# Forty-eight products of the identity at the head of TensorE's program for the experts

## The reference

```python
x = x + xattn(layernorm(x), ctx, Wq, Wk, Wv, Wo, bo)      # 16 heads of 64
x = x + causal_attention(layernorm(x), wq, wk, wv, wo)    # 16 heads of 64
y = layernorm(x)
probs = softmax(y @ router)                               # 8 experts
top, idx = top_k(probs, 2); gates = softmax(top)
for each token and each of its two experts e:
    h = silu(y @ gate[e]) * (y @ up[e])                   # 256 -> 512
    x += gates * (h @ down[e])                            # 512 -> 256
```

## Time and profile before

| | us |
|---|---|
| median of three runs | 2300.44 (2297.36 to 2302.71) |
| the profiled execution | 2298.02 |
| its span, first to last instruction | 2296.3 |
| TensorE busy in it | 2176.0 (95%) |
| VectorE, ScalarE, GpSimd busy | 1555.2, 1301.2, 914.2 |
| third stage, from 1925.92 | 370.4 |

### The profile page before, as it was taken

One profiled execution on the slowest core, in us unless ns is written; L12 is line 12 of the kernel. 1 busy time (PEld: TensorE's weight loads), 2 busy tenths in 40 slices (PEclk: granted clock), 3 DMA queues, 4 the chain that ended last, 5 costly groups with the idle time before them and its releaser, 6 DMA issues. The chain is left out here.

```text
span 2296.3 us, 56727 instructions
## 1 busy us (share of the span) xinstructions
PE 2176.0 (95%) x19008; PEld 1980.3 (86%) x19008; DVE 1555.2 (68%) x3525; ACT 1301.2 (57%) x3925; POOL 914.2 (40%) x1409
## 2 busy tenths in 40 slices
PE   6999999999999999999996999999999994999996
PEld 5899999999999999999995899999999983888885
DVE  6666676767676666667654888888888874444442
ACT  5555555555555555555553777777677762545442
POOL 3333333333333333333332225555555554444443
PEclk9999999999999999999997999999999996999998
DMA  4000000000000000000005200000000003444434
GB/s 120 22 20 28 9 27 18 27 11 25 27 18 27 9 27 18 27 9 27 14 6 172 104 11 16 22 21 19 23 19 21 22 25 105 100 82 97 81 63 108
DMA packets 63901, 93.55 MB, mean 41 GB/s; under 512 B 6824, under 2 KB 47144, under 8 KB 63528
## 3 DMA queue, kind: packets, MB, share of 16 engines
q1 hardware_dynamic: 44280, 64.49, 8.8%
q0 software_dynamic: 13104, 18.56, 4.6%
q10 hardware_dynamic: 6432, 9.44, 1.4%
HBM read 65.39 MB, written 36.83 MB: 45 GB/s over the span
## 5 line engine op out<-in xcount | busy, mean ns | idle before, releaser
L424 POOL TENSOR_TENSOR p_sb<-p_sb,rinv 128x512 f32<-128x512 f32 x256 | 279.0, 1090 | 780.0 <-DVE rinv L770 780.0
L679 ACT ACTIVATE p_sb<-s_ps,nmax 128x256 f32<-128x256 f32 x512 | 238.1, 470 | 198.7 <-DVE nmax L745 194.9
L745 DVE TENSOR_REDUCE nmax<-s_ps 128x2 f32<-128x512 f32 x256 | 176.1, 688 | 186.1 <-PE s_ps L67 181.7
L1090 POOL TENSOR_TENSOR sp_sb<-sp_sb,srinv 128x512 f32<-128x512 f32 x128 | 133.1, 1040 | 228.8 <-DVE srinv L1444 226.7
L1340 ACT ACTIVATE sp_sb<-sm_sb,snmax 128x128 f32<-128x128 f32 x512 | 199.6, 391 | 5.6 <-DVE snmax L1459 2.6
L767 DVE COPY pt_sb<-t_ps 128x512 f32<-128x512 f32 x256 | 176.8, 690 | 22.2 <-PE t_ps L567 8.4
L48 ACT ACTIVATE q_sb<-m_ps 64x256 fp32r<-64x256 f32 x256 | 96.8, 378 | 164.4 <-PE m_ps L67 160.6
L47 ACT CAST qk_hi<-qk_ps 128x512 fp32r<-128x512 f32 x218 | 129.6, 595 | 95.6 <-PE qk_ps L67 87.7
L567 PE MATMUL t_ps<-ident,p_sb 128*128 128x128 f32 x1024 | 153.6, 273 | 2.1 <-POOL p_sb L424 1.1
L67 PE MATMUL sqk_ps<-e_w_hi 128*128 128x256 f32 x512 | 147.8, 289 | 7.2 <-DVE e_w_lo L59 7.2
L567 PEld LDWEIGHTS t_ps<-ident,p_sb 128*128 128x128 f32 x1024 | 125.1, 141 | 31.6 <-issue 4.4
(11 more groups left out here) (340 smaller groups left out, 7465.7 us busy)
## 6 DMA issues: line engine op xcount, KB each, us to landing
e_xs_in<-xs SPq DMA_DIRECT2D x69, 132.5 KB, 2.1
ctx_raw<-in_ctx_t SPq DMA_DIRECT2D x32, 256.0 KB, 2.8
ctx_raw<-in_ctx_t SPq DMA_DIRECT2D x64, 128.0 KB, 2.9
xs<-blank_rows SPq DMA_DIRECT2D x8, 662.5 KB
x_ring<-in_x SPq DMA_DIRECT2D x16, 256.0 KB, 2.8
x_mid<-x_ring SPq DMA_DIRECT2D x16, 256.0 KB, 2.2
acc<-x_sb SPq DMA_DIRECT2D x16, 256.0 KB, 2.1
out_x<-acc SPq DMA_DIRECT2D x8, 512.0 KB, 5.3
```

Source lines behind the costliest of these rows:

```text
L424: nc.gpsimd.tensor_tensor(prob, prob, inv, ALU.mult).then_inc(norm_done, 1)
L679: ex = nc.scalar.activation(p_sb[:, k, b * J:(b + 1) * J], s_ps[1 - w][:, b * J:(b + 1) * J], ACT.Exp, bias=nmax[:, k, b:b + 1], scale=1.0 ...
L745: nc.vector.tensor_reduce(nmax[:, (p - 1) % 4, :], s_ps[1 - w][:].rearrange("p (b j) -> p b j", b=2), AX_X, ALU.max, negate=True).then_inc ...
L1090: nc.gpsimd.tensor_tensor(prob, prob, inv, ALU.mult).then_inc(norm_done, 1)
```

## The change

Ahead of turn_x(0), TensorE multiplies the identity by itself 48 times, into the first 128 columns of y_ps, each product complete in itself. Nothing waits for them, they wait for nothing, and nothing reads what they write: down(0) starts y_ps anew.

```diff
@@ -1867,6 +1867,8 @@
                     gate_up(i, w)
                     down(before, w_before)
 
+                for k in range(48):
+                    pe.matmul(y_ps[:, 0:P], ident[:], ident[:], start=True, stop=True)
                 turn_x(0)
                 turn_x(1)
                 pe.wait_ge(s_wlo, PIECES)
```

## The result

The changed kernel is slower by 0.41%: median 2309.84 us (2304.89 to 2311.66, 8 runs) against 2300.72 us (2296.03 to 2304.95, 8 runs) of the kernel before on the same chip, a ratio of 1.0041 with a 95% interval of 1.0032 to 1.0050, or +7.4 to +11.5 us.

A forecast was written before the change was run, and what follows sets the result against it. The prediction took TensorE's chain, busy in 95% of the span, to bound the kernel. A delay of 10.4 us less 2.8 us back gave +7.6 us, a median of 2308.0 us (+0.33%), range 2302 to 2314.

The forecast's parts named there:

- No slack behind the head of the stage: Experts' stage: whatever delays turn_x(0) or gate_up(0) delays the end; tiles follow every 5.08 us, additions 4.94 us apart.
- Where the products start: Head of the experts' stage: products start at the barrier's release, 1925.92 us, with 2.51 us of pause open before turn_x(0).
- rival 4: Products run ahead of the barrier in the 23 us pause; at best 2.8 us gained, 2297.6 us; chance 0.04.
- How many: Added block: the 48 plain float32 products become 96 matmuls, each with its own weight load.
- Rival 1: Added block: one matmul a product, 0.107 us cold, 0.059 warm; -0.5 us, 2299.9 us; chance 0.07.
- The price: Added block: weight load and movement side by side, 0.213 us a matmul cold and 0.113 warm.
- Rival 2: Added block: load and movement in turn, 0.32 us a matmul cold, 0.168 warm; +12.9 us, 2313.3 us; chance 0.10.
- The rise of the clock: Added block: clock rises 4.3 us in, the middle of 2.7 and 5.9; block 12.9 us, turn_x(0) 10.4 later.
- Rival 3: Added block: clock does not rise on this work; +18.0 us, nothing back, 2318.4 us; chance 0.11.
- What comes back: turn_x(0) to the end of gate_up(0): warm it takes 4.96 us instead of 7.78, so 2.8 us come back.
- The sum: Whole kernel: +10.4 us of delay less 2.8 us back gives +7.6 us, between +6.3 and +8.5.
- The rule beside it: Added block: the skill's 107 ns throttled, 56 ns full clock per 128-column product; 48 cost 4.7 to 5.1 us, nearly free.

The follow-up runs named there:

- e4_cols8: Changed kernel with its 48 identity products moving 8 columns instead of 128, all weights still loaded; one run, 2319.32 us.
- e5_w16: Changed kernel with its 48 products loading 16 weight columns instead of 128, still moving 128 columns; one run, 2312.2 us.
- e10_24_early: Changed kernel with 24 products instead of 48 and the second expert's three weight transfers moved to the stage before; 2304.53 us, ratio 1.0025 to the kernel before.
- e8_tail72_10: Changed kernel with 72 products at the end of the stage before and 10 instead of 48 at the experts' head; 2298.22 us, ratio 1.0001 to the kernel before.
- e3_f32r: Changed kernel with 48 float32r products of the experts' weights, one matmul each, instead of the float32 identity; 2306.83 us against 2301.18 of the kernel before, ratio 1.0028.
- e13_early: Kernel before, without products, with only the second expert's three weight transfers moved to the stage before; 2300.23 us, ratio 1.0000.
- e11_tail78_10_early: Changed kernel with 78 products in the stage before, 10 at the experts' head, second expert's weight transfers moved earlier; 2297.56 us, ratio 0.9998 to the kernel before.

## Why the prediction was right

Forecast: a median of 2308.0 us, between 2302 and 2314, slower with 0.84; measured 2309.84. By its steps:

- **No slack behind the head of the stage.** Right. Tiles and additions kept their pace, and the 7.7 us that turn_x(2) was late are in the end of the chain.
- **Where the products start.** Right: at the barrier's release, as ScalarE does (1929.18 and 1929.14), so rival 4 (ahead of the barrier) falls. The pause hid 2.5 us of them.
- **How many.** 96 matmuls. Rival 1 (one pass each) falls.
- **The price.** From 1929.18 to 1933.00 the stretches count 18 matmuls, 0.212 us each (forecast 0.213); from 1934 to 1941, on the higher clock, 63 in 7.00 us, 0.111 to 0.113 each (forecast 0.113). The bounds came from rows with the same load but little movement, and the prediction put the movement at 0.107 us cold. It measured 0.213, the same as the load (e4_cols8, e5_w16). That it is no more than the load, and lies beside it, is why the price still met: in this the forecast was lucky. Rival 2 (in turn) falls.
- **The rise of the clock.** 4.75 us after the start, forecast 4.3, the middle of two far ends. (The nearer end was misread: 0.69 in the earlier trace rows puts that rise at 1253.6, 2.9 us after the work began and not 2.7, which moves the middle by 0.1 us.) Across the runs with such products the rise came 3.2 (e10_24_early) to 5.1 us (e8_tail72_10) after the first, either of which would have moved the length of the block by some 0.5 us; that this run lay near the middle is partly chance. 0.45 us more at the lower clock cost 0.45 x (1 - 0.113/0.213) = 0.2 us. With this the block ended 13.2 us after the start of the stage, forecast 12.9. Rival 3 (the clock stays down) falls for this work, and only for it: in e4_cols8 it came true, with +16.5 us where the rival said +18.0, and in e3_f32r too the clock stayed down to the end of the block. Its chance of 0.11 was no formality: that the clock rises on unbroken work, which the forecast took for granted, is not so for all work.
- **What comes back.** 3.0 us, forecast 2.8; turn_x(0) itself was warm in 0.38 us.
- **The sum.** +7.7 us in the trace (+7.4 in the second run of the change), forecast +7.6.

The medians say more, +9.1 and +9.3 us, with intervals that reach down to 7.4 and 6.9. The rest I can't place: the start of the stage (1925.3 to 1931.7 us) and the time behind turn_x(2) (355 to 360 us) scatter by some us between single profiled executions, that of e13_early, which has no products, among them. Whether 1 to 2 us of the cost lie outside the stretch that I compared stays open.

**The rule beside it.** The Trainium skill (TensorE: Matmul & The Clock Gate, Back-to-back issue gap), read as one pass of 128 columns a product, put the 48 at 4.7 to 5.1 us as an estimate; the block took 13.3. The trace disagrees: 0.213 and 0.113 us for each of two matmuls.

**What the sum did not hold.** It was right for 48 products and would have been wrong for 24: by the same terms +2.3 us, measured +6.3 in the trace. The hold is a term that the prediction did not have. In the change the first signal of TensorE came after 13 us, later than any that was held in these runs, and nothing in the prediction had foreseen that this matters: that was luck.

## What to carry to other kernels

Products put at the head of a stage to raise the clock are paid on the chain, past the pause that is open there, and bring back at most what the first steps lose on the lower clock (2.8 to 3.0 us here): count the matmuls that a product becomes, price load and movement apart and take the larger, and set the block against the open pause before adding one. If they are wanted, put them in the pause ahead of the barrier and only a handful behind it; in this kernel that gained 3 us of 2300 in one trace, which the time did not confirm, and nothing in a near twin of it (e8_tail72_10). And test more than one size: the cost went -0.8, +6.3, +7.7 us for 12, 24 and 48 products, not in proportion.

## What was not expected of the hardware

- The granted clock did not rise for every unbroken work: it stayed at 0.50 through 20.6 us of float32 matmuls with 8 moved columns and through 10.5 us of float32r matmuls of 128 columns, and rose 3.2 to 5.1 us into float32 matmuls of 128 moved columns, 4.6 us into those with 16 weight columns and 4.2 us into transposes. The rows tell which did and which did not, not why.
- A silence of 1.85 us at the barrier was followed by a fall of the clock, 1.2 us into the next products (e8_tail72_10); one of 1.65 us was not (e11_tail78_10_early). One trace of each, and the second kernel also has more products ahead of the barrier and its transfers moved.
- Signals of TensorE to other engines came 1.1 to 2.7 us late in four kernels, and 0.3 us late in a fifth, when they were raised 7.4 to 9.6 us after the start of the stage; cause open.
